# Two-layer transformer block on one core: row sums of attention over added pairs of key tiles

## The reference

```python
x = x + attention(layernorm(x)) @ W_out + b_out      # 16 heads of 32, causal, softmax(q k / sqrt(32)) v
x = x + (silu(h @ W_gate.T) * (h @ W_up.T)) @ W_down.T   # h = layernorm(x), hidden size 2048
```

## Time and profile before

| | us |
|---|---|
| median of 3 runs | 2178.95 (2174.32 to 2179.26) |
| the profiled execution | 2179.44 |
| its span, first to last instruction | 2177.7 |
| TensorE busy (matmuls) | 2113.8, 97% |
| VectorE busy | 1253.6, 58% |
| GpSimd busy | 668.9, 31% |
| ScalarE busy | 530.9, 24% |

### The profile page before, as it was taken

The page is one execution under the profiler, slowest core; times in us unless marked ns, Lnnn a source line. Parts: engine busy times, 40 slices in busy tenths (PEclk is TensorE's granted clock), DMA queues, the critical chain, the costliest instruction groups (busy, mean ns, idle before and its releaser), DMA issues.

```text
span 2177.7 us, 34223 instructions
## 1 busy us (share of the span) xinstructions
PE 2113.8 (97%) x11056; PEld 1486.4 (68%) x11056; DVE 1253.6 (58%) x2476; ACT 530.9 (24%) x1076; POOL 668.9 (31%) x508
## 2 busy tenths in 40 slices
PE   6999999999999999999989999999999999999998
PEld 5555478888755548888865554888877554588886
DVE  6766564544676647444467665644456767454445
ACT  1344420000144441000014454100011444310001
POOL 3324233332312323323231233333323223233322
PEclk9999999999999999999999999999999999999999
DMA  4333111111323211111242321111113232111113
GB/s 130 94 79 79 31 36 52 49 58 39 79 70 79 70 31 49 50 48 49 68 129 70 79 69 40 39 59 39 49 40 81 68 81 68 40 49 49 59 39 97
DMA packets 59748, 135.15 MB, mean 62 GB/s; under 512 B 10784, under 2 KB 11808, under 8 KB 59552
## 3 DMA queue, kind: packets, MB, share of 16 engines
q1 hardware_dynamic: 59552, 132.71, 21.6%
HBM read 77.62 MB, written 4.19 MB: 38 GB/s over the span
## 4 chain that ended last, share of the span: by engine, by line
PE 88%; issue 5%; DVE 2%; POOL 2%; ACT 1%; DMA 1%; SPq 0%; DVEq 0%; POOLq 0%; ACTq 0%
PE ring L898 13%; PE ring L899 13%; PE ring L900 13%; PE bank L1011 13%; PE ring L965 8%; PE bank L989 7%; PE bank L898 7%; PE bank L900 7%; PE bank L899 7%; PE ring L889 1%; ACT prob L560 1%; DMA area<-nm_lo 1%; POOL area L438 1%; DVE xn L699 1%; POOL prob L463 1%
## 5 line engine op out<-in xcount | busy, mean ns | idle before, releaser
L898 PE MATMUL ring<-xt_hi,area 128*128 128x512 f32 x1248 | 489.8, 392 | 1.1 <-DVE kq_parts L688 1.1
L899 PE MATMUL ring<-xt_lo,area 128*128 128x512 f32 x1248 | 486.4, 390 | 0.0
L900 PE MATMUL ring<-xt_hi,area 128*128 128x512 f32 x1248 | 486.0, 389 | 0.0
L699 DVE CUSTOM_DVE_ANT_0 xn<-ring,mask_row 128x128 bf16<-128x128 f32 (+7 forms) x512 | 374.5, 749 | 99.9 <-PE ring L965 93.9
L560 ACT ACTIVATE prob<-bank 128x512 f32<-128x512 f32 (+3 forms) x768 | 335.0, 489 | 342.4 <-PE bank L989 341.6
L436 POOL TENSOR_SCALAR area<-w_stage 128x1024 fp32r<-128x1024 f32 x131 | 144.4, 1103 | 762.2 <-PE bank L900 404.7
L766 DVE TENSOR_TENSOR prob<-prob,ring 128x512 f32<-128x512 f32 x128 | 87.8, 686 | 456.9 <-ACT prob L578 456.9
L438 POOL TENSOR_TENSOR area<-w_stage,area 128x1024 fp32r<-128x1024 f32 x131 | 322.8, 2464 | 10.9
L578 ACT ACTIVATE prob<-ring 128x512 f32<-128x512 f32 x128 | 76.5, 598 | 970.4 <-PE ring L900 970.4
L898 PEld LDWEIGHTS ring<-xt_hi,area 128*128 128x128 f32 x1248 | 234.3, 188 | 59.1 <-issue 9.8
L900 PEld LDWEIGHTS ring<-xt_hi,area 128*128 128x128 f32 x1248 | 234.3, 188 | 49.1
(11 more groups left out here) (78 smaller groups left out, 2053.4 us busy)
## 6 DMA issues: line engine op xcount, KB each, us to landing
w_stage<-ffn_w SPq DMA_DIRECT2D x96, 512.0 KB, 3.3
area<-kq_parts SPq DMA_DIRECT2D x336, 128.0 KB, 2.4
w_stage<-attn_w SPq DMA_DIRECT2D x35, 512.0 KB, 3.3
x<-x_in SPq DMA_DIRECT2D x24, 256.0 KB, 3.9
area<-attn SPq DMA_DIRECT2D x48, 128.0 KB, 2.3
out<-x SPq DMA_DIRECT2D x16, 256.0 KB, 2.2
bias_rows<-row_bias SPq DMA_DIRECT2D x10, 256.0 KB, 4.2
area<-nm_hi SPq DMA_DIRECT2D x32, 8.0 KB, 1.8
```

What stands on the lines that cost most here:

```text
L699: dve.tensor_tensor_reduce(out=sum_out[:, RING[name] % 2, 0:keys], in0=src[:, 0:keys], in1=mask_row[:, TOKENS - keys:], scale=1.0, scalar= ...
L898: pe.matmul(dst, ah, bh, start=first and k == 0, stop=False)
L899: pe.matmul(dst, ah, bl, start=False, stop=False)
L900: ins = pe.matmul(dst, al, bh, start=False, stop=last and k == n - 1)
```

## The change

- In the eight-tile units the exps of key tiles 0 and 1, 2 and 3, 4 and 5 are added by GpSimd, the second onto the first in place, after the values group of the first has been issued. Each add comes in two parts of two heads. One sums group is run for a pair, and one each for tiles 6 and 7: five groups for eight tiles. Four-tile units keep one group for each tile.
- The sums group of pair (0,1) stands in step j = 3, of (2,3) in j = 5, of (4,5) in j = 7, directly ahead of that of tile 6. The adds stand in GpSimd's order by `ADDS_AT`, behind the mask of the same step.
- `prob` has four buffers. The exps of a step wait for the values group of the step four before, and for its sums or its add.
- VectorE splits attention outputs 5, 6 and 7, each directly after its multiply. GpSimd splits 0 and 1 within unit 5 (j = 1, j = 5), 2 and 4 ahead of unit 6's masks, 3 at the end of unit 6.
- The copy of one element after `split_max` goes; the subtraction that writes `nm_lo` frees the ring buffer, and SyncE waits for that.
- The five pieces of unit 6 stand at the points 0, 2, 5, 7, 10 (before 0, 2, 4, 6, 10).
- The scratch area for DMA descriptors is 1024 bytes.

The diff, cut to its core:

```diff
@@ points(u) @@
     if u == UNITS - 2:
-        return [0, 2, 4, 6, 10]
+        n = len(beside(u))
+        return [i * 10 // (n - 1) for i in range(n)]
@@ constants @@
+PROB_BUFS = 4
+PAIRED = (0, 6)
+ADD_PARTS = 2
+def sums_in(u, j):
+    return [group for group in sum_groups(u)[:-1] if j == (group[-1] + 2 if len(group) == 2 else group[0] + 1)]
+ADDS_AT = ({}, {1: (((0, 1), 0), ((0, 1), 1)), 3: (((2, 3), 0),), 4: (((2, 3), 1),), 5: (((4, 5), 0),), 6: (((4, 5), 1),)})
+POOL_SPLITS = UNITS - 3
+SPLIT_ORDER = (0, 1, 2, 4, 3)
+def sum_groups(u):
+    paired = PAIRED[unit(u)[1]]
+    return [(j, j + 1) for j in range(0, paired, 2)] + [(j,) for j in range(paired, key_tiles(u))]
...
-        prob = sb("prob", [P, 2, GH, CHUNK])
+        prob = sb("prob", [P, PROB_BUFS, GH, CHUNK])
@@ sync: stack_max @@
-                wait_alone(sp, max_split, it * UNITS + u + 1)
+                wait_alone(sp, ring_drained, drained(it, ("mt", u)))
@@ gpsimd @@
+            def add_pair(it, u, pair, part):
+                first, second = pair
+                step = J_BASE[u] + second
+                d = second - CT * unit(u)[1]
+                off = max(0, d) * P
+                heads = slice(part * GH // ADD_PARTS, (part + 1) * GH // ADD_PARTS)
+                wait_alone(pool, prob_ready, it * S2_STEPS + GH * (step + 1))
+                if d >= 0:
+                    wait_alone(pool, mask_done, it * UNITS * CT + u * CT + d + 1)
+                wait_alone(pool, pv_done, it * KEY_STEPS + J_BASE[u] + first + 1)
+                dst = prob[:, (step - 1) % PROB_BUFS, heads, off:]
+                pool.tensor_tensor(dst, dst, prob[:, step % PROB_BUFS, heads, off:], ALU.add).then_inc(pair_added, 1)
...
-                    if u == UNITS - 1:
-                        for w in range(UNITS - 3, UNITS - 1):
-                            split_attn(it, w)
                     if u in SPLIT_BEFORE:
                         split_weights(it, SPLIT_BEFORE[u])
-                    if u == UNITS - 3:
-                        for w in range(UNITS - 3):
+                    for w in {6: (2, 4)}.get(u, ()):
+                        split_attn(it, w)
+                    for j in range(key_tiles(u)):
+                        if j >= CT * unit(u)[1]:
+                            mask_probs(it, u, j - CT * unit(u)[1])
+                        for pair, part in ADDS_AT[unit(u)[1]].get(j, ()):
+                            add_pair(it, u, pair, part)
+                        for w in {(5, 1): (0,), (5, 5): (1,), (6, 3): (3,)}.get((u, j), ()):
                             split_attn(it, w)
-                    for d in range(CT):
-                        mask_probs(it, u, d)
-                        if u == UNITS - 1 and d == 0:
+                        if u == UNITS - 1 and j == CT:
                             inverse_deviation(it, 1, 0)
@@ scalar: exps @@
-                    if step >= 2:
-                        act.wait_ge(pv_done, it * KEY_STEPS + step - 1)
+                    if step >= PROB_BUFS:
+                        w, i = step_of(step - PROB_BUFS)
+                        group = group_of(w, i)
+                        act.wait_ge(pv_done, it * KEY_STEPS + step - PROB_BUFS + 1)
+                        if i == group[0]:
+                            act.wait_ge(sums_done, summed(it, w, group))
+                        else:
+                            act.wait_ge(pair_added, added(it, w, group))
@@ vector @@
-                                             ALU.subtract).then_inc(max_split, 1)
-                    dve.wait_ge(max_split, it * UNITS + u + 1)
-                    dve.tensor_copy(row_max[0:1, u % 2, 0:1], row_max[0:1, u % 2, 0:1]).then_inc(ring_drained, 1)
+                                             ALU.subtract).then_inc(ring_drained, 1)
...
                                 normalise_attn(u - 1)
+                                if u - 1 >= POOL_SPLITS:
+                                    split_last(u - 1)
...
                 normalise_attn(UNITS - 2)
+                split_last(UNITS - 2)
@@ tensor @@
+                def sums(u, group):
+                    j = group[0]
+                    step = J_BASE[u] + j
+                    off = max(0, j - CT * unit(u)[1]) * P
+                    if len(group) == 2:
+                        pe.wait_ge(pair_added, added(it, u, group))
+                    for h in range(GH):
+                        rows = slice(h * HEAD, (h + 1) * HEAD)
+                        ins = pe.matmul(den_bank[rows, off:], ones[:, :], prob[:, step % PROB_BUFS, h, off:],
+                                        start=j == 0, stop=group == sum_groups(u)[-1], tile_position=(0, h * HEAD))
+                    ins.then_inc(sums_done, 1)
...
-                                else:
-                                    weigh(u, j - 1, what)
+                                elif half == 0:
+                                    weigh(u, j - 1)
+                                else:
+                                    for group in sums_in(u, j):
+                                        sums(u, group)
```

More of the change, by code:

```diff
@@ L157, with step_of, group_of @@
 S2_STEPS = GH * KEY_STEPS
+PROB_BUFS = 4
[9 more added lines that the diff above has]
+    return [(j, j + 1) for j in range(0, paired, 2)] + [(j,) for j in range(paired, key_tiles(u))]
+SUM_ORDER = [(u, group) for u in range(UNITS) for group in sum_groups(u)]
+PAIR_ORDER = [(u, group) for u, group in SUM_ORDER if len(group) == 2]
+SUMS, PAIRS = len(SUM_ORDER), len(PAIR_ORDER)
+def step_of(step):
+    u = max(v for v in range(UNITS) if J_BASE[v] <= step)
+    return u, step - J_BASE[u]
+def group_of(u, j):
+    return next(group for group in sum_groups(u) if j in group)
 ROWS = STEPS * CT
@@ L301, in buffer_free, with summed, added @@
             return it * RING_USES + RING[name] - 1 + RING_CREDIT
+        def summed(it, u, group):
+            return it * SUMS + SUM_ORDER.index((u, group)) + 1
+        def added(it, u, group):
+            return ADD_PARTS * (it * PAIRS + PAIR_ORDER.index((u, group)) + 1)
         def stacked(it, u, each):
@@ L559, in exps @@
                         act.wait_ge(s2_full, it * S2_STEPS + n + 1)
[L560 removed]
+                        act.activation(prob[:, step % PROB_BUFS, h, off:], bank[n % 2][:, off:], ACT.Exp,
                                        scale=SCALE).then_inc(prob_ready, 1)
@@ L990, in scores_t, with weigh @@
                               q_stack[rows, q_buffer(u), h, off:], start=True, stop=True).then_inc(s2_full, 1)
-                def weigh(u, j, what):
+                def weigh(u, j):
                     g, c = unit(u)
@@ L998, in weigh @@
                     off = max(0, d) * P
-                    if what == "values":
-                        pe.wait_ge(prob_ready, it * S2_STEPS + GH * (step + 1))
-                        if d >= 0:
-                            pe.wait_ge(mask_done, it * UNITS * CT + u * CT + d + 1)
-                        if j == 0 and not u:
-                            pe.wait_ge(side_taken, side_done(it, ("k", 2)))
-                        if j == 0 and u:
-                            pe.wait_ge(evacuated, it * UNITS + u)
+                    pe.wait_ge(prob_ready, it * S2_STEPS + GH * (step + 1))
@@ L1007, in weigh @@
+                    if d >= 0:
+                        pe.wait_ge(mask_done, it * UNITS * CT + u * CT + d + 1)
+                    if j == 0 and not u:
+                        pe.wait_ge(side_taken, side_done(it, ("k", 2)))
+                    if j == 0 and u:
+                        pe.wait_ge(evacuated, it * UNITS + u)
                     for h in range(GH):
                         rows = slice(h * HEAD, (h + 1) * HEAD)
-                        dst, a = ((out_bank, v[:, j, g * P + h * HEAD:g * P + (h + 1) * HEAD]) if what == "values"
-                                  else (den_bank, ones[:, :]))
@@ L1011, in weigh @@
-                        ins = pe.matmul(dst[rows, off:], a, prob[:, step % 2, h, off:], start=j == 0,
+                        ins = pe.matmul(out_bank[rows, off:], v[:, j, g * P + h * HEAD:g * P + (h + 1) * HEAD],
+                                        prob[:, step % PROB_BUFS, h, off:], start=j == 0,
                                         stop=j == key_tiles(u) - 1, tile_position=(0, h * HEAD))
-                    if what == "sums":
-                        ins.then_inc(pv_done, 1)
+                    ins.then_inc(pv_done, 1)
@@ L1024, in project_out @@
                         if t == 0:
-                            pe.wait_ge(attn_split, it * (UNITS - 1) + UNITS - 3)
+                            pe.wait_ge(attn_split, it * POOL_SPLITS + SPLIT_ORDER.index(4) + 1)
                             pe.wait_ge(w_split, it * SLOTS + WO_SLOT0 + 2)
-                    if t == 0 and groups[-1] == GROUPS - 1:
-                        pe.wait_ge(attn_split, it * (UNITS - 1) + UNITS - 1)
-                    if t == CT and groups[-1] == GROUPS - 1:
```

(15 more changed lines are left out.)

25 lines of the change are left out of this document (13 added, 12 removed).

## The result

The changed kernel takes 2197.68 us (median of 4 runs, 2195.75 to 2203.7) against 2177.73 us for the kernel before (median of 4). The ratio is 1.0097, 95% interval 1.0079 to 1.0114: 20 us slower, above the range of the prediction (2156 to 2191). The profiled execution took 2199.39 us with a span of 2197.6.

A forecast was written before the change was run, and what follows sets the result against it. TensorE, busy for 97% of the span, was taken as the bound. Per iteration +1.5 (units 1, 3, 5) + 0.2 (unit 7) - 1.4 (unit 6) = +0.3 us, four iterations 1.2 us: 2178 us, range 2156 to 2191.

The forecast's parts named there:

- Units 1 and 3: Units 1, 3 and 5: skipped sums groups win about 0.5 us a unit, 1.5 us an iteration, 6 us in four.
- Each shift: Unit 1: values groups after the skipped sums at j=1, 2, 4 come earlier, 0.5, 1.1, 1.7 us kept.
- the loss at j=6: Unit 1, step j=6: the next scores wait for the 1024-wide maximum, so nothing of the skipped group is kept.
- Rival 1: Units 1, 3, 5: VectorE's spare time absorbs its backlog, half of 3.2 us kept each; 2159 us, chance 0.33.
- GpSimd's adds: Eight-tile units: add parts take 2.4 and 1.85 us, 13.3 us a unit; sums wait under 0.3 us for them.
- Rival 3: Eight-tile units: slow adds make each pair's sums wait about 1 us; 2197 us, chance 0.06.
- Unit 7: Unit 7: skipped groups save time, GpSimd's chain takes most back; 0.2 us won an iteration, between -1 and +1.2.
- Unit 6: Unit 6: loses 0.5 (transpose of maxima), 0.8 (scores' wait), 0.1 (splits before masks): 1.4 us an iteration, between 0 and 3.
- 1.5 + 0.5 of cover against 1.0 + 1.15: Before unit 7's scores: cover and later TensorE against later maximum and output 5's split; a wait near 0.3 us.
- the sign of a right working: Unit 7's first scores wait for the maxima's DMA by under 1 us in the profile after.
- rival 2: End of unit 6: VectorE and GpSimd exclude each other, 2.7 us lost an iteration; 2188 us, chance 0.19.
- The copy and the exp buffers: Dropping the copy after the maxima's split brings 0 to 2 us; four exp buffers free nothing by themselves.

The follow-up runs named there:

- repaired kernels: Changed kernel with output 5 split behind the maxima's split, old points, outputs 2 and 4 split between unit 6's masks: 2177.48 us with pairs, 2176.30 us without.
- fourth experiment: Changed kernel without pairs, with splits and points as before; four exp buffers and the missing copy stay: 2177.59 us, ratio 1.0004.
- dense start: Second output projection dealt out around unit 7's first scores: repaired kernel 2169.08 us; no pairs, old splits and points 2173.05; changed kernel with extra matmuls 2187.36.

## Why the prediction was wrong, point by point

**Units 1 and 3: right, unit 5 less.** Predicted 0.5 us a unit; units 1-2 are 0.46 us shorter, 3-4 0.5. Each shift came out about as walked (0.4, 0.8 and 1.3 us kept in front against 0.5, 1.1 and 1.7), with the loss at j=6. Unit 5 gave less: between the repaired kernels with and without pairs mid differs by 0.05 us, and the kernels with pairs wait there longer for the DMA of the maxima in some iterations (0.4 to 1.2 us, mostly in the third and fourth), the kernels without never did. No term of the prediction had that, and its cause stays open. Rival 1 (half of 3.2 us kept) fell: the ring buffers and the exps come last there, whatever VectorE's share says.

**GpSimd's adds: right in size.** The line of the adds in the changed kernel, least, median and longest ns:

```profile
L523 POOL TENSOR_TENSOR prob<-prob x96: 1818/2371/2553, 98.5 to 1906.6; 128x1024 f32<-128x1024 f32 x64, 128x768 f32<-128x768 f32 x32
```

2.4 and 1.85 us were predicted from the weights' subtraction. The sums waited 3.0 us for them in all, 0.7 at the longest, where I had set 0.3; four of the five waits are in unit 7. Rival 3 named 2197 us, nearly what was measured, but by a mechanism that isn't there: the adds aren't slow and their removal leaves units 1 and 3 as they were. A time that fits shows no mechanism.

**Unit 7: right.** Predicted 0.2 us won, measured 0.33 in the one iteration at full clock.

**Unit 6: a term too small.** Predicted 1.4 us an iteration, of it 0.5 for the transpose of maxima (its wait is 0.48) and 0.8 in front of the scores; the second measured 1.94. Units 5 and 6 with the hold were to lose 0.9 us together and lost 2.6. (Before the engines' meeting the prediction's own terms, 1.5 + 0.5 of cover against 1.0 + 1.15, leave a wait of 0.15 and not 0.3.) Two things were missed. The scores wait 0.18 us for the DMA, under the 1 us that I had named as the sign of a right working, and the sign misled: the time is lost one step earlier, on the second output projection, through the ring buffer that the maxima sit in: I followed the maxima to their reader by DMA and not the buffer to its next writer. And GpSimd's weight split came in right behind output 3: its copy at 242.25 ran to 243.47, and VectorE's subtraction ended only at 244.00. Only the split of output 3 was in my working. This is rival 2, which I gave 0.19: its cast ended at 244.5 (242.57 measured) and its subtraction at 245.2 (244.00), but its 2.7 us a unit is what was lost (0.66 + 1.94 = 2.6, with unit 5 in it). The Trainium skill, page SBUF — State Buffer, section Who interferes with whom, has GpSimd and such VectorE instructions (two SBUF inputs, or a cast in a two-port mode) exclude each other for a whole instruction. The trace agrees roughly, with the cast at 1.33 us instead of 0.43: it ended 0.29 us behind GpSimd's instruction, a little less than its usual length.

**The clock: no term at all.** This is the step that failed, more than unit 6. The page showed a 9 in every slice, and I took the clock as given. Yet unit 7 of the second and third iteration of before took 35.2 us instead of 33.65, so two falls were there to be read, and rows of one iteration could not show them. At full clock the change costs 5 us, 7 with the DMA of unit 5, which my range would have held; falls bring 13 to 14 more, and with them it costs 20.

**The rest: right.** The copy and the exp buffers bring nothing (fourth experiment). The points were priced at 0.5 us an iteration, and mid shows 0.58 (47.36 against 46.78); the splits ahead of the masks at 0.1, and it is 0.3.

**What stays open** is what exactly decides a fall. Counted over the profiled executions of all kernels, unit 7 has a fall in 15 of 20 iterations where hold is 7.75 us, in 5 of 24 where it is 5.81, and in none of 12 with the dense start. Filling the 1.55 us stop did not help (4 of 4), so it stays open what else of the longer hold does it. In units 1, 3 and 5 the kernels with pairs have 8 falls in 108 units, each 1.0 to 2.1 us behind the stop of about 0.78 us; without pairs there is no such stop, and no fall in 60 units. So a dense start of unit 7 keeps the clock up there, and the pairs' own stop can bring it down, but mostly doesn't. Whether that stop can be closed wasn't tried.

## What to carry to other kernels

Where TensorE bounds a kernel, work taken from it is worth only what the next waits leave, and the gap that stays in its place can cost as much as the work did, as with the pairs in the repaired kernel: read the granted clock of short windows in every iteration, not the slices of the page. When VectorE gets work in front of a small result, follow the buffer that holds that result to its next writer, and list all that GpSimd then has ready, since each of its instructions can hold VectorE up (a cast took 1.33 us instead of 0.43). A light stretch of TensorE is the place for independent matmuls: the same projection, dealt out between scores, was worth 7 to 8 us.

## What the runs showed of the hardware

In the attention units the clock fell to its lower level behind stops of 0.2 to 1.57 us (0.78 us in unit 3 of the repaired kernel). At the start of unit 7 the last two stops before a fall are 0.45 and 0.21 us, in the kernel before as in the changed one. At 252 us of the changed kernel the clock was at 0.55 while TensorE was busy for 6.74 of 7 us. A values group took 1.88 us there instead of 1.06.

The Trainium skill, page TensorE: Matmul & The Clock Gate, section HAM oscillation — how this bites in real kernels, lays such falls to waits for DMA that are longer than the work between them. Ahead of these falls no run shows such a wait: the DMA waits at unit 7 are 0.2 us, and the longest ahead of a fall, 1.52 us at unit 5, is far shorter than the work around it. The page's next section, A second HAM failure mode: psum-queue depth-cycling, has short idle moments between groups of matmuls do the same in another kernel, and that is what these traces agree with.
